# A fused attention and feed-forward kernel: its last stage in 15 turns instead of 16, output writes that wait for a pair of tokens' blocks, and a new order of the last two groups

## The reference

```
x = x + attn16(layernorm(x), ctx)            # 16 heads, 77 keys, softmax, out projection
x = x + layernorm2(n + relu(n@w1+b1)@w2+b2)  # n = layernorm(x); 1024 hidden, expert 0 alone
x = x + attn1(layernorm(x), layernorm(ctx))  # one head over the 77 keys
x = x + route(layernorm(x))                  # below
```

```
scores = pe(S) @ sign(tile_sigs).T
idx    = argmax(scores, axis=-1)                    # one of 8 per position
out[b, s] = n[b, s] @ W[idx[s]].T + bias[idx[s]]
```

## Time and profile before

| what | value |
|---|---|
| time, median of 3 | 275.23 us |
| runs | 276.38, 275.23, 274.96 us |
| span of the profiled execution, first to last instruction | 272.0 us |
| PE busy | 249.2 us, 92% |
| DVE busy | 220.3 us, 81% |
| POOL busy | 189.7 us, 70% |
| ACT busy | 160.7 us, 59% |
| granted clock of PE, mean | 0.982 |

### The profile page before, as it was taken

The page is one execution under the profiler, slowest core; times in us unless marked ns, Lnnn a source line. Parts: engine busy times, 40 slices in busy tenths (PEclk is TensorE's granted clock), DMA queues, the critical chain, the costliest instruction groups (busy, mean ns, idle before and its releaser), DMA issues.

```text
span 272.0 us, 6214 instructions
## 1 busy us (share of the span) xinstructions
PE 249.2 (92%) x2048; PEld 221.2 (81%) x2048; DVE 220.3 (81%) x573; ACT 160.7 (59%) x510; POOL 189.7 (70%) x361
## 2 busy tenths in 40 slices
PE   1969899899799999999999999999999997989990
PEld 1758676699798879998898799989899996867880
DVE  2899999999998889954999985898587589976551
ACT  3559795864363868695385896457645173465430
POOL 3367788987958896775497788878785497427354
PEclk9995999999999999999999999999999999999997
DMA  6992020011101182000002321121160000000032
GB/s 175 329 326 89 0 81 0 2 39 42 39 2 40 41 265 86 14 9 2 0 2 63 76 77 42 58 60 40 57 217 2 0 0 2 0 2 2 39 154 116
DMA packets 11156, 17.61 MB, mean 65 GB/s; under 512 B 1377, under 2 KB 7509, under 8 KB 11125
## 3 DMA queue, kind: packets, MB, share of 16 engines
q1 hardware_dynamic: 9333, 11.98, 13.9%
q0 software_dynamic: 1792, 5.24, 6.4%
HBM read 14.07 MB, written 3.15 MB: 63 GB/s over the span
## 4 chain that ended last, share of the span: by engine, by line
PE 68%; DVE 15%; POOL 5%; ACT 5%; issue 4%; DMA 1%; SPq 0%; POOLq 0%; DVEq 0%; ACTq 0%
PE PB L266 29%; PE PB L259 12%; PE PB L464 9%; PE S L387 5%; PE PB L339 5%; PE PB L399 4%; PE S L377 4%; ACT E L1066 2%; DVE SX L659 2%; POOL E L1263 1%; DMA WKV<-in_w_k 1%; DVE SX L673 1%; POOL SM L1220 1%; DVE HL L686 1%; DVE XTL L638 1%
## 5 line engine op out<-in xcount | busy, mean ns | idle before, releaser
L1263 POOL TENSOR_TENSOR E<-E,SX 128x308 f32<-128x308 f32 x64 | 43.8, 712 | 10.7 <-DVE SX L676 10.4
L1066 ACT ACTIVATE E<-S,SX 128x77 f32<-128x77 f32 x128 | 39.4, 336 | 10.6 <-DVE SX L659 10.6
L266 PE MATMUL PB<-XTH,W1H 128*128 128x256 f32 x128 | 37.7, 295 | 1.5 <-DVE XTL L638 1.4
L266 PE MATMUL PB<-W2H,HH 128*128 128x256 f32 x128 | 37.6, 294 | 0.0
L266 PE MATMUL PB<-XTL,W1H 128*128 128x256 f32 x128 | 36.2, 283 | 0.0
L266 PE MATMUL PB<-XTH,W1L 128*128 128x256 f32 x128 | 36.2, 282 | 0.0
L266 PE MATMUL PB<-W2H,HL 128*128 128x256 f32 x128 | 35.5, 278 | 0.0
L266 PE MATMUL PB<-W2L,HH 128*128 128x256 f32 x128 | 35.5, 278 | 0.0
L1220 POOL TENSOR_TENSOR SM<-SM,nhalf 128x2 f32<-128x2 f32 x40 | 28.3, 707 | 3.1
L1089 ACT ACTIVATE HH<-PB 128x512 fp32r<-128x512 f32 x32 | 19.0, 598 | 18.0 <-PE PB L266 18.0
L1076 ACT ACTIVATE EW<-S 124x640 f32<-124x640 f32 x32 | 21.9, 711 | 10.9 <-PE S L387 10.1
(11 more groups left out here) (203 smaller groups left out, 725.2 us busy)
## 6 DMA issues: line engine op xcount, KB each, us to landing
RAW<-in_w SPq DMA_DIRECT2D x4, 512.0 KB, 6.3
WD<-in_WD SPq DMA_DIRECT2D x8, 256.0 KB, 4.6
X<-in_x SPq DMA_DIRECT2D x4, 256.0 KB, 5.4
x<-X SPq DMA_DIRECT2D x4, 256.0 KB, 2.1
E<-in_WD SPq DMA_DIRECT2D x4, 256.0 KB
bc<-in_rows SPq DMA_DIRECT2D x1, 640.0 KB, 5.6
X<-in_w1r SPq DMA_DIRECT2D x1, 512.0 KB, 6.6
RT<-in_WD SPq DMA_DIRECT2D x2, 256.0 KB, 2.9
```

What stands on the lines that cost most here:

```text
L266: t = e.matmul(dst, a, b, start=first and j == 0, stop=last and j == n - 1)
L1066: t = e.activation(Ei[:, h * NK:(h + 1) * NK], P[:, at:at + NK], ACT.Exp, bias=SX[:, i, 0, k:k + 1], accum_out=SX[:, i, 1, k:k + 1])
L1263: t = e.tensor_tensor(Eh, Eh, SX[:, i, 2, 8 * a + h:8 * a + h + 4].unsqueeze(2).to_broadcast([128, 4, NK]), ALU.mult)
```

## The change

Three things, in one edit.

The turns of the last stage are 15. The first twelve are still two pairs of one batch. Pairs 12, 13 and 14 are done for both batches in one turn each. The order of the turns is no longer batch 0's first four, batch 1's first four, then in turn; it is (batch, pairs): 0: 0-1, 0: 2-3, 0: 4-5, 0: 6-7, 0: 8-9, 1: 0-1, 0: 10-11, 1: 2-3, 1: 4-5, 1: 6-7, 1: 8-9, 1: 10-11, both: 12, both: 13, both: 14.

The counter `pa` counts pairs instead of turns. `put(m)` waits for pair m + 7 of both batches, `pa` waits for the pair before it in its own batch, and `pr`'s bank is free after the turn's two pairs.

```diff
-        TURNS = [(b, r) for b in range(2) for r in range(4)] + [(b, r) for r in range(4, 8) for b in range(2)]
-        TURN = {br: k for k, br in enumerate(TURNS)}
+        def pairs_in(k):
+            r = k // 2 if k < 12 else k
+            b = k % 2
+            return [(b, 2 * r), (b, 2 * r + 1)] if k < 12 else [(0, k), (1, k)]
+
+        TURNS = [pairs_in(k) for k in (0, 2, 4, 6, 8, 1, 10, 3, 5, 7, 9, 11, 12, 13, 14)]
+        TURN = {bn: k for k, turn in enumerate(TURNS) for bn in turn}
+        ADDED = {bn: k + 1 for k, bn in enumerate(bn for turn in TURNS for bn in turn)}
...
-            def pr(b, r, p):
-                w.wait_ge(s["pc"], TURN[b, r] + 1)
-                P = hold(("pr", b, r), ("B", p), ("pa", TURN[b, r] + 1))
+            def pr(k, p):
+                w.wait_ge(s["pc"], k + 1)
+                P = hold(("pr", k), ("B", p), ("pa", 2 * k + 2))
...
-            def pa(b, r):
-                w.wait_ge(s["pr"], TURN[b, r] + 1)
-                w.wait_ge(s["bd"], 4 * b + min(r, 3) + 1)
-                w.wait_ge(s["pa"], TURN[b, r])
-                P = bank("pr", b, r)
+            def pa(k):
+                w.wait_ge(s["pr"], k + 1)
+                P = bank("pr", k)
+                for v, (b, n) in enumerate(TURNS[k]):
+                    w.wait_ge(s["bd"], 4 * b + min(n // 2, 3) + 1)
+                    if n:
+                        w.wait_ge(s["pa"], ADDED[b, n - 1])
...
             def put(m):
-                w.wait_ge(s["pa"], TURN[1, (m + 7) // 2] + 1)
+                w.wait_ge(s["pa"], max(ADDED[0, m + 7], ADDED[1, m + 7]))
```

More of the change, by code:

```diff
@@ L968, in vector @@
             hl(0, 3); apply("B", 1); lo("A", 3); r_pairs(); lo("B", 1); ssum(2, 1, 1); ql(3); y(0); stats("A", 4)
[L969 to L992, removed]
+            smax(3, 0, 0); smax(3, 0, 1); hl(1, 0); apply("A", 4); stats("Y", 0); f_q(); hl(1, 1); x2(0); ssum(3, 0, 0)
@@ new lines, in vector @@
+            ssum(4, 0, 1); lo("B", 3); ssum(4, 1, 0); cm(0); ssum(4, 1, 1); apply("C", 1); starts(); y(2); hl(3, 0)
+            stats("Y", 2); smax(5, 0, 1); hl(3, 1); x2(2); stats("C", 2); hl(3, 2); hl(3, 3); x1(4); smax(5, 1, 0)
+            ssum(5, 0, 0); stats("B", 4); smax(5, 1, 1); cm(1); ssum(5, 0, 1); ssum(5, 1, 0); ssum(5, 1, 1)
+            apply("C", 2); y(3); lo("A", 6); apply("A", 7); stats("Y", 3); x3_(0); x2(3); ql(6); stats("C", 3); cm(2)
+            apply("B", 4); x3_(1); apply("C", 3); smax(6, 0, 0); smax(6, 0, 1); lo("A", 7); x1(5); smax(6, 1, 0)
@@ new lines, in vector @@
+            lo("B", 4); stats("B", 5); ql(7); ssum(6, 0, 0); x3_(2); cm(3); smax(6, 1, 1); ssum(6, 0, 1); hl(4, 0)
+            hl(4, 1); hl(4, 2); apply("B", 5); ssum(6, 1, 0); hl(4, 3); x3_(3); ssum(6, 1, 1); lo("B", 5); smax(7, 0, 0)
+            smax(7, 0, 1); y(4); stats("Y", 4); x2(4); stats("C", 4); hl(5, 0); hl(5, 1); stats("D", 0); hl(5, 2)
+            smax(7, 1, 0); hl(5, 3); ssum(7, 0, 0); ssum(7, 0, 1); apply("D", 0); smax(7, 1, 1); apply("C", 4); x1(6)
+            stats("B", 6); ssum(7, 1, 0); stats("D", 1); ssum(7, 1, 1); y(5); stats("Y", 5); apply("B", 6)
@@ new lines, in vector @@
+            apply("D", 1); x2(5); lo("B", 6); cm(4); stats("C", 5); x1(7); hl(6, 0); stats("D", 2); hl(6, 1); hl(6, 2)
+            stats("B", 7); hl(6, 3); apply("C", 5); stats("D", 3); pa(0); apply("B", 7); apply("D", 2); x3_(4)
+            apply("D", 3); stats("D", 4); cm(5); lo("B", 7); y(6); stats("Y", 6); hl(7, 0); x2(6); hl(7, 1); hl(7, 2)
+            hl(7, 3); x3_(5); stats("C", 6); stats("D", 5); apply("D", 4); apply("C", 6); y(7); stats("Y", 7); x2(7)
+            stats("C", 7); cm(6); apply("C", 7); pa(1); pa(2); cm(7); x3_(6); apply("D", 5); stats("D", 6); pa(3)
@@ L994, in scalar @@
+            apply("D", 6); pa(4); x3_(7); stats("D", 7); pa(5); apply("D", 7); pa(6); pa(7); pa(8); pa(9); pa(10)
+            pa(11); pa(12); pa(13); pa(14)
         def scalar(e):
@@ L1161, in gpsimd @@
+            cpt(6); pc(5); apply("D", 5); cex(7); cpt(7); pc(6); apply("D", 6); xtd(5); xtd(6); pc(7); pc(8)
+            apply("D", 7); xtd(7); pc(9); pc(10); pc(11); pc(12); pc(13); pc(14)
         def gpsimd(e):
```

141 lines of the change are left out of this document (66 added, 75 removed).

## The result

| | before | after |
|---|---|---|
| time, median of 20 | 275.13 us (274.02 to 276.38) | 273.16 us (271.76 to 275.65) |
| ratio | | 0.9942 [0.9922, 0.9961] |
| span of the profiled execution | 272.0 us | 272.7 us |
| granted clock of PE in it | 0.982 | 0.975 |

The change makes the kernel faster, by 0.6%, just past what can be told from no change. But the executions of after fall into two groups by their mean granted clock: 12 with 0.979 to 0.988 took 271.8 to 273.7 us (median 272.2), and 8 with 0.971 to 0.975 took 273.9 to 275.7 (median 274.95). I call the second kind the low-clock executions. The times of before show no such groups. The profiled execution is one of the eight (274.57 us), so its span is even longer than that of before.

The account below looks back on a forecast made before the run. PE, busy 92% of the span, was taken as the bound. PE's end 263.3 + 1.7 to write 7 + 4.28 = 269.3 against 272.0, so 275.23 - 2.7 = 272.5 us; range 270.9 to 274.7.

Parts of the forecast that it names:

- the colliding pair of `x2(7)`: Two DVE operations ahead of norm C of group 7 take 1.70 us beside POOL's adds `bd(4)`, against 0.88 alone.
- Start of `tD(3)`: On PE, `tD(3)` waits for `hl(7, 3)`, behind `hh(7, 3)`, not `hl(7, 2)`: starts at 224.85, 1.2 us earlier.
- From `tD(3)` to PE's end: On PE, 35.4 us of work plus 3.05 of idle, 4.0 before; PE ends at 263.3, 2.1 us earlier.
- the 1.5 us that I let `tC(7)` wait: PE idles 1.5 us ahead of `tC(7)`, which needs norm C of group 7 and starts at 238.0.
- The sign that I gave: PE's wait of about 1.5 us ahead of `tC(7)` ends with ACT's apply.
- The writes: Eight writes queued on POOL 1.265 us apart; write 7 starts 1.7 us after PE's end, not 2.32: 0.6 us gained.
- the 3.2 us between span and median: Before: profiled span 272.0 against timed median 275.23 us; the difference was carried over unchanged.
- DVE was not full: Rival, DVE from 236 to 249.6: busy 12.5 of 13.6 us, PE loses 1.3 to 1.5 more, 274.0; chance 0.20.
- The collision did happen: Rival, `bd(4)` beside `x2(7)`: collision absent or hidden, `tC(7)` 0.8 us earlier, 271.4; chance 0.17.
- A whole add of waiting for each L710: Rival at `x2(7)`: each operation waits for a whole POOL add, `tC(7)` another 0.65 us later, 273.1; chance 0.08.
- Group 7's first norm: Rival, ahead of `w1(7, 0)` on PE: norm B comes too late; 277 at 5.3 us of delay; chance 0.12.
- The writes alone: Rival: PE's end stays and only the writes gain, 0.6 us, 274.6; counted with the full-DVE rival's upper end.

Follow-up runs that it names:

- the second profile of the changed kernel: The changed kernel run once more, nothing altered: median 273.86 us of 12, ratio 0.9943; the profiled execution took 271.82 us at the higher clock.
- Taking the collision away: Against the changed kernel, `bd(4)` on POOL goes back behind `rs("C", 7)`: median 271.74 us of 6, ratio 0.9886; repeated, 271.53 us, ratio 0.9883.
- the writes by turn: Changed kernel, but write m waits as before for pairs up to the odd one at or behind m + 7: median 274.9 us of 12, ratio 0.995.
- turn 4 ahead and `bd(4)` back: Changed kernel with turn 4 moved ahead of `tC(7)` on PE and `bd(4)` behind `rs("C", 7)` on POOL: median 274.43 us of 12, ratio 0.9981.
- fillers: Unread matmuls on PE: three ahead of `tC(7)` in the changed kernel, 272.59 us; two ahead of `cp(7)` with turn 4 ahead and `bd(4)` back, 273.01 us.

## Why the prediction was right

*The time.* 272.5 was forecast, 273.16 measured; the 12 executions at the higher clock have 272.2. That the median of all 20 lies so near is in part luck: the sum holds for the executions without the fall, and the median depends on how many had it. With 6 of 12 it was 273.86, only 0.9 us below the kernel before beside it, where 2.7 was forecast. The parts of the sum, in the second profile of the changed kernel less its late start of 0.42:

| step | predicted | measured |
|---|---|---|
| `tD(3)` starts | 224.85 | 224.99 |
| the colliding pair of `x2(7)` | 1.70 | 1.75 |
| `tC(7)` starts | 238.0 | 237.96 |
| PE ends | 263.3 | 263.3 |
| write 7 behind PE's end | 1.7 | 1.98 |
| from there to the end | 4.28 | 4.29 |

*Start of `tD(3)`.* Right, with its reason: it hangs on `hh(7, 3)`, as the run with adds beside `x2(6)` shows: `tD(3)` kept its distance from `hh(7, 3)` while `x2(6)` took 1.3 us more.

*From `tD(3)` to PE's end.* Right. Of the 1.5 us that I let `tC(7)` wait the trace lists 1.15; I counted from starts and it counts from modelled ends. Counted from starts it is 1.34 (two turns from 233.57, 3.47 us by the price of a row, and 238.38). The sign that I gave, that the wait ends with ACT's half of the norm, came true. The small waits for ACT and DVE went, but for 0.2. Taking the collision away gave 0.9 us of PE's time on the common scale, and 1.6 to 2.3 us of the median, since the low clock went with it.

*The writes.* The mechanism was right (a closed queue), its size was off: write 0 starts 6.94 before PE's end, not 7.15, and the first interval is 1.35, not 1.265; seven of them take 8.92. So the term gives 0.34 and not 0.6.

*What the prediction missed.* First, the clock. I priced the new wait at its own length, and in 14 of 32 executions it cost more: in the profile of after, `co(6)` and turn 4 took 0.82 and 0.91 us longer than in the second profile, 1.7 in all, of which 1.3 reached PE's end. In the profile with the writes by turn (0.972) it was 2.7. Between the medians of the two groups lie 2.75 us; both kinds of fall are in it, and the spread of the start. It moved the median from the 272.2 of the higher clock to 273.16 in the first 20 runs, and from 272.36 to 273.86 in the next 12. Second, the 3.2 us between span and median that I carried over were 1.85 around the span and 1.3 to 1.4 by which the one profiled execution was faster than the median; its `tD(1)` at 199.67 is the earliest of all profiles here, so an early start is the likely reason. It did no harm, since the other executions of after spread in the same way.

*The rivals.* DVE was not full: PE waits for L755 or L736 nowhere, and DVE was busy for 11.1 of the 13.6 us, not the 12.5 of that rival. In the changed kernel, that is; with turn 4 ahead and `bd(4)` back an add did hold PE for 0.3. The collision did happen. It cost 0.87 us for two instructions against two adds. A whole add of waiting for each L710 would have been 1.46. The rule of "SBUF — State Buffer" of the Trainium skill ("Who interferes with whom"), read as a lock for the whole instruction, is thus the upper bound here and not the price: 1.70, 1.75 and 1.72 for a pair with adds beside it, 0.88 without. Group 7's first norm was in time: no wait ahead of `w1(7, 0)`. "The writes alone" as a bound (274.6, 0.6 us less) was too dear: without any of the new order they give 1.1 to 1.3 us.

*What stays open.* Why the same wait of 1.15 us brings the clock down in some executions and not in others, and costs more in one than in another. And the spread of the start, up to 2.2 us in the profiles: the same eight matmuls of two programs that don't differ there took 2.09 and 3.41 us in the chain, with a granted clock of 1.00 in the records and the DMA engines busy for 0.9 to 1.1 of the time. No run was made on it.

## What to carry to other kernels

Price a new wait on TensorE twice: at its length, and at a stretch of matmuls behind it at half the clock, which here cost 1.3 or 2.7 us of PE's end when it came; where the wait can't be removed, matmuls that nobody reads were a cheap cover here. Look at single executions and their clocks, not at the median alone. When you move work into a wait, look at what that work had been covering. And when a VectorE operation with two SBUF inputs stands on the path, put no independent GpSimd adds beside it. Where it has slack, they do no harm: such a collision cost 0.9 us at one place and nothing at the other.

## What was new about the hardware

- With a wait of 1.15 us ahead of the short matmuls of `tC(7)` the mean clock was low in 20 of 44 executions (the changed kernel, and it with the old waits of the writes), with one of 2.5 us in 6 of 6, with one of 0.3 in none of 12, and with fillers in none of 14. With one of 1.2 us at another place it was low in none of 12 in one kernel and in 4 of 65 in another.
- The fall of the clock behind the same wait cost PE's end 1.3 us in one profile and 2.7 us in another.
- Two VectorE operations with two SBUF inputs each (128x256, fp32) took 1.70 to 1.75 us beside GpSimd adds of the same size, and 0.88 without.
- GpSimd issued the indirect writes that were already released every 1.265 us (0.96 busy, 0.30 between); the first interval was 1.35. The program ended 4.28 us after the last issue in before, 4.24 and 4.29 after the change.
